# A graph kernel in three sweeps: the joint between the first and the second rearranged

## What is computed

```
h  = relu(layernorm(x))
x  = x + (adj.T @ h) * inv_deg[:, None]      # inv_deg = 1 / column sums of adj, infinite -> 0
h  = relu(layernorm(x))
x1 = silu((adj @ h)  @ W + b)
x2 = silu((adj @ x1) @ W + b)
out = x + x2
```

## Time and profile before

| | us |
|---|---|
| median of 3 runs | 663.56 (662.71 to 665.02) |
| the profiled execution | 661.49 |
| its span in the trace | 659.7 |
| busy: PE / DVE / POOL / ACT | 626.2 / 520.9 / 571.3 / 302.0 |

### The profile page before, as it was taken

One profiled execution on the slowest core, in us unless ns is written; L12 is line 12 of the kernel. 1 busy time (PEld: TensorE's weight loads), 2 busy tenths in 40 slices (PEclk: granted clock), 3 DMA queues, 4 the chain that ended last, 5 costly groups with the idle time before them and its releaser, 6 DMA issues.

```text
span 659.7 us, 6763 instructions
## 1 busy us (share of the span) xinstructions
PE 626.2 (95%) x2212; PEld 401.7 (61%) x2212; DVE 520.9 (79%) x518; ACT 302.0 (46%) x376; POOL 571.3 (87%) x287
## 2 busy tenths in 40 slices
PE   4989999999997889899999999999999999998996
PEld 2356666666564545566666666666666666665664
DVE  3988799999966879687777787787777978965982
ACT  1484442733623254646445445445435435443452
POOL 2399899599695958998999999999999999996994
PEclk9989999999998898999999999999999999999999
DMA  8999999999999699999999999909999999999971
GB/s 275 353 373 343 333 349 351 322 329 341 337 280 294 225 240 346 347 329 319 325 345 333 335 346 320 312 16 175 287 345 346 343 316 344 341 307 293 319 249 32
DMA packets 155826, 199.80 MB, mean 303 GB/s; under 512 B 5520, under 2 KB 138896, under 8 KB 155792
## 3 DMA queue, kind: packets, MB, share of 16 engines
q1 hardware_dynamic: 90512, 135.02, 65.6%
q10 hardware_dynamic: 65280, 64.36, 33.5%
HBM read 197.26 MB, written 2.10 MB: 302 GB/s over the span
## 4 chain that ended last, share of the span: by engine, by line
PE 60%; POOL 21%; issue 11%; DMA 3%; DVE 2%; ACT 1%; SPq 1%; ACTq 0%; POOLq 0%; DVEq 0%
PE dg L375 22%; POOL a_lo L738 14%; PE dg L392 10%; PE dg L381 10%; PE dg L382 10%; POOL at_lo L752 6%; PE m_ps L301 3%; PE m_ps L401 2%; DMA h<-in_x_dram 2%; DMA raw<-in_adj_dram 1%; DVE dg L591 1%; PE m_ps L306 1%; POOL norm L719 1%; PE m_ps L307 1%; PE m_ps L319 1%
## 5 line engine op out<-in xcount | busy, mean ns | idle before, releaser
L752 POOL TENSOR_TENSOR at_lo<-turned,at_hi 128x1024 fp32r<-128x1024 f32 x160 | 379.8, 2414 | 20.4 <-ACT at_hi L489 15.1
L634 DVE STREAM_TRANSPOSE turned<-raw 128x1024 f32<-128x1024 f32 x256 | 302.6, 1222 | 83.3 <-PE dg L375 40.3
L489 ACT ACTIVATE at_hi<-turned 128x1024 fp32r<-128x1024 f32 x160 | 168.6, 1059 | 196.1 <-DVE turned L634 137.6
L738 POOL TENSOR_TENSOR a_lo<-raw,a_hi 128x1024 fp32r<-128x1024 f32 x66 | 155.3, 2390 | 34.8 <-ACT a_hi L459 34.4
L375 PE MATMUL dg<-turned,f_w 128*128 128x512 f32 x384 | 181.6, 595 | 2.5 <-DVE turned L634 1.9
L591 DVE TENSOR_TENSOR dg<-raw,dg 128x2048 f32<-128x2048 f32 x60 | 137.5, 2291 | 26.2 <-DMA raw<-in_adj_dram 23.3
L381 PE MATMUL dg<-at_hi,f_hi 128*128 128x512 f32 x320 | 133.2, 416 | 4.1 <-ACT at_hi L489 4.0
L392 PE MATMUL dg<-at_lo,f_hi 128*128 128x512 f32 x320 | 130.2, 488 | 2.3 <-POOL at_lo L752 2.1
L382 PE MATMUL dg<-at_hi,f_lo 128*128 128x512 f32 x320 | 126.4, 395 | 0.0
L301 PE MATMUL m_ps<-raw,h 128*128 128x512 f32 x248 | 114.0, 606 | 10.0 <-ACT h L434 8.6
L375 PEld LDWEIGHTS dg<-turned,f_w 128*128 128x128 f32 x384 | 72.9, 190 | 58.0 <-issue 49.8
(11 more groups left out here) (48 smaller groups left out, 255.6 us busy)
## 6 DMA issues: line engine op xcount, KB each, us to landing
raw<-in_adj_dram SPq DMA_DIRECT2D x64, 1024.0 KB, 7.4
raw<-in_adj_dram ACTq DMA_DIRECT2D x122, 512.0 KB, 13.2
raw<-in_adj_dram SPq DMA_DIRECT2D x118, 512.0 KB, 12.1
x<-in_x_dram SPq DMA_DIRECT2D x16, 128.0 KB, 7.5
out_dram<-zs SPq DMA_DIRECT2D x12, 128.0 KB, 12.6
h<-in_x_dram SPq DMA_DIRECT2D x1, 768.0 KB, 9.4
h<-in_x_dram SPq DMA_DIRECT2D x1, 256.0 KB, 3.4
out_dram<-zs SPq DMA_DIRECT2D x4, 64.0 KB, 1.9
```

The lines of the kernel that those rows point to most:

```text
L489: act.activation(at_hi[:, s % RING3], turned[:, unit % TURN], ACT.Copy).then_inc(hi3_done, 1)
L634: dve.transpose(dst, src).then_inc(t3_done, 1)
L738: pool.tensor_tensor(a_lo[:, s % RING1], raw1[:, v % RAW1, i], a_hi[:, s % RING1].bitcast(f32), ALU.subtract).then_inc(lo1_done, 1)
L752: pool.tensor_tensor(at_lo[:, s % RING3], turned[:, unit % TURN], at_hi[:, s % RING3].bitcast(f32), ALU.subtract).then_inc(lo3_done, 1)
```

## The change

- WHOLE1_LAST: in the last quarter pairs 12 and 14 are whole too, so that nothing is split behind pair 11 (v = 59). In pair1 the last pair then has no rest of the pair before, and main1 takes over the end of the sum and the semaphore half_done; copy_message waits for main1_done as well.
- Memory: a_hi, a_lo, h_hi and h_lo now lie in front of raw1, and piece buffers 1 and 2, at_hi and at_lo lie over them. Pieces 1 and 2 wait for the last split pair alone (main1_done 60, its low parts, its rest1); piece 3 waits for pair 61.
- Piece 0 is issued in four places: block 0 by SP behind the load of v=53, block 1 behind that of v=55, block 2 by ScalarE behind hi1(53), block 3 behind hi1(56).
- ScalarE, behind the last split pair: its halves of pieces 1 and 2, then the rounding of units 1 and 2 (AHEAD3), then relu2(2) and the message copies; its half of piece 3 behind unit 1. GpSimd: scale_shift(2), the low parts of units 1 and 2, then lo_h2(2). GpSimd's scale_shift(2) stood behind lo1(62) before.
- The last quarter's turn_message comes behind units 1 and 7 on PE instead of 0 and 6; on DVE invert moves from unit 5 to 7, add_message from 6 and 10 to 8 and 12, node_statistics from 7 and 11 to 9 and 13.
- invert keeps the sum, its reciprocal and the comparison's result in PSUM (tp), and only the clamped value and the final inverse in SBUF.
- PE makes RISE = 14 multiplies of 128 x 128 by 128 columns, whose results nobody reads, before the first pair.

The diff, with fewer lines around each edit:

```diff
--- before.py
+++ after.py
@@ -13,9 +13,11 @@
 RAW1 = 5
+RISE = 14
 RING1 = 5
 WHOLE1 = (0, 1, 4, 7, 10, 13, 15)
+WHOLE1_LAST = (0, 1, 4, 7, 10, 12, 13, 14, 15)
 WHOLE1_FIRST = (0, 1, 2, 3, 4, 5, 7, 10, 13, 15)
@@ -41,6 +43,8 @@
 EARLY3 = (60, 61, 62, 63)
+AHEAD3 = (1, 2)
+PIECE0_SP, PIECE0_ACT = (53, 55), (53, 56)
 KEPT = range(SWEEP2, SWEEP2 + RAW3)
@@ -80,29 +84,31 @@
         norm = sb("norm", [P, 4, NT])
-        deg = sb("deg", [P, 5, QT])
+        deg, inv_deg = sb("deg", [P, QT]), sb("inv_deg", [P, QT])
         sweep1, sweep2 = ExitStack(), ExitStack()
-        raw1 = sb("raw1", [P, RAW1, 2, QC], into=sweep1)
         a_hi = sb("a_hi", [P, RING1, QC], f32r, into=sweep1)
         a_lo = sb("a_lo", [P, RING1, QC], f32r, into=sweep1)
-        h = sb("h", [P, NT, P], into=sweep1)
         h_hi = sb("h_hi", [P, 2 * len(SPLIT_ROWS), P], f32r, into=sweep1)
         h_lo = sb("h_lo", [P, 2 * len(SPLIT_ROWS), P], f32r, into=sweep1)
+        raw1 = sb("raw1", [P, RAW1, 2, QC], into=sweep1)
+        h = sb("h", [P, NT, P], into=sweep1)
         msgT = sb("msgT", [P, QC], into=sweep1)
-        raw3 = {n: sb(f"raw3_{n}", [P, GB, BC], into=sweep2) for n in (1, 2, 3)}
+        raw3 = {n: sb(f"raw3_{n}", [P, GB, BC], into=sweep2) for n in (1, 2)}
+        at_hi = sb("at_hi", [P, RING3, UC, GROUP], f32r, into=sweep2)
+        at_lo = sb("at_lo", [P, RING3, UC, GROUP], f32r, into=sweep2)
+        spare = sb("spare", [P, 512], into=sweep2)
+        raw3[3] = sb("raw3_3", [P, GB, BC], into=sweep2)
         f3_hi = sb("f3_hi", [P, UC * len(SPLIT3), P], f32r, into=sweep2)
         f3_w = sb("f3_w", [P, UC * len(WHOLE3), P], into=sweep2)
-        at_hi = sb("at_hi", [P, RING3, UC, GROUP], f32r, into=sweep2)
-        at_lo = sb("at_lo", [P, RING3, UC, GROUP], f32r, into=sweep2)
         nT = sb("nT", [P, 2, QC], into=sweep2)
         zs = sb("zs", [P, 2, QT, P], into=sweep2)
-        gap = sb("gap", [P, 3 * 1024], into=sweep2)
+        gap = sb("gap", [P, 5 * 512], into=sweep2)
         raw3[0] = sb("raw3_0", [P, GB, BC], into=sweep2)
@@ -150,7 +156,7 @@
         def whole1(v):
-            return v % PAIRS in (WHOLE1_FIRST if v < PAIRS else WHOLE1)
+            return v % PAIRS in {0: WHOLE1_FIRST, QUARTERS - 1: WHOLE1_LAST}.get(v // PAIRS, WHOLE1)
@@ -204,11 +210,15 @@
-            if i in (1, 2, 3):
-                pairs = QUARTERS * PAIRS - (2 if i == 1 else 0)
-                eng.wait_ge(main1_done, pairs)
-                eng.wait_ge(lo1_done, 2 * split_before(pairs))
-                eng.wait_ge(deg_added, pairs)
+            if i in (1, 2):
+                eng.wait_ge(main1_done, splits1[-1] + 1)
+                eng.wait_ge(lo1_done, 2 * len(splits1))
+                eng.wait_ge(rest1_done, len(splits1))
+            elif i == 3:
+                eng.wait_ge(main1_done, QUARTERS * PAIRS - 2)
+                eng.wait_ge(deg_added, QUARTERS * PAIRS - 2)
             elif i >= RAW3:
@@ -264,6 +274,8 @@
                 load1(v)
+                if v in PIECE0_SP:
+                    load3(sp, 0, SP_BLOCKS[PIECE0_SP.index(v):][:1])
                 if v % PAIRS in NODES_AT:
@@ -298,7 +310,8 @@
                     if whole1(v):
-                        mm = pe.matmul(acc, h[:, 2 * k + i], raw1[:, v % RAW1, i, cols], start=first, stop=False)
+                        last = k == PAIRS - 1 and i == 1 and whole1(v - 1)
+                        mm = pe.matmul(acc, h[:, 2 * k + i], raw1[:, v % RAW1, i, cols], start=first, stop=last)
                     else:
@@ -307,6 +320,8 @@
                     mm.then_inc(main1_done, 1)
+                elif k == PAIRS - 1 and whole1(v - 1):
+                    mm.then_inc(half_done, 1)
@@ -329,7 +344,8 @@
                         main1(v, half)
-                        rest1(v - 1, half)
+                        if before:
+                            rest1(v - 1, half)
                 else:
@@ -403,6 +419,9 @@
             pe.wait_ge(consts_ready, 1)
+            for _ in range(RISE):
+                pe.matmul(tp[:, 0, 0:P], ident[:, :], ident[:, :], start=True, stop=True)
             for v in range(QUARTERS * PAIRS):
@@ -414,9 +433,9 @@
                     rest3(unit - 1)
-                if unit == 0:
+                if unit == 1:
                     turn_message(QUARTERS - 1, 0)
-                if unit == 6:
+                if unit == 7:
                     turn_message(QUARTERS - 1, 1)
@@ -462,6 +481,7 @@
                 act.activation(turned_nodes(msgT[:, :], 0), natural(m_ps[:, 0:512]), ACT.Copy).then_inc(msgT_copied, 1)
+                act.wait_ge(main1_done, (q + 1) * PAIRS)
                 act.wait_ge(rest1_done, split_before((q + 1) * PAIRS))
@@ -481,7 +501,7 @@
                 if s == 0:
-                    act.wait_ge(main1_done, QUARTERS * PAIRS)
+                    act.wait_ge(main1_done, splits1[-1] + 1)
                     act.wait_ge(rest1_done, len(splits1))
@@ -526,17 +546,20 @@
                     relu2(v // PAIRS - 2)
-                if v // PAIRS == QUARTERS - 1 and v % PAIRS == 6:
-                    load3(act, 0, SP_BLOCKS + ACT_BLOCKS)
+                if v in PIECE0_ACT:
+                    load3(act, 0, ACT_BLOCKS[PIECE0_ACT.index(v):][:1])
+            load3(act, 1, ACT_BLOCKS)
+            load3(act, 2, ACT_BLOCKS)
+            for unit in AHEAD3:
+                hi3(unit)
             relu2(QUARTERS - 2)
-            load3(act, 1, ACT_BLOCKS)
             copy_message(QUARTERS - 1)
             for unit in range(UNITS3):
-                if not whole3(unit):
+                if not whole3(unit) and unit not in AHEAD3:
                     hi3(unit)
                 i = unit // QU + RAW3 - 1
-                if unit in (1, 2):
-                    load3(act, unit + 1, ACT_BLOCKS)
+                if unit == 1:
+                    load3(act, 3, ACT_BLOCKS)
                 if unit % QU == 0 and RAW3 <= i < len(PIECES) and i not in KEPT:
@@ -598,12 +621,13 @@
             def invert(q):
-                inv, clamped, finite, inv_deg = (deg[:, n, :] for n in range(4))
+                total, inv, finite = (tp[:, 1, n * QT:(n + 1) * QT] for n in range(3))
+                clamped = deg[:, :]
                 dve.wait_ge(msg_turned, 3 * q + 1)
-                step(dve.reciprocal(inv, tp[:, 1, 0:QT]))
+                step(dve.reciprocal(inv, total))
                 step(dve.tensor_scalar(clamped, inv, -FLT_MAX, FLT_MAX, ALU.max, ALU.min))
                 step(dve.tensor_tensor(finite, inv, clamped, ALU.is_equal))
-                dve.tensor_tensor(inv_deg, clamped, finite, ALU.mult).then_inc(inv_ready, 1)
+                dve.tensor_tensor(inv_deg[:, :], clamped, finite, ALU.mult).then_inc(inv_ready, 1)
@@ -614,7 +638,7 @@
                     ins = dve.scalar_tensor_tensor(out=row, in0=tp[:, part, m * P:(m + 1) * P],
-                                                   scalar=deg[:, 3, k:k + 1], in1=row, op0=ALU.mult, op1=ALU.add)
+                                                   scalar=inv_deg[:, k:k + 1], in1=row, op0=ALU.mult, op1=ALU.add)
                 ins.then_inc(u_ready, 1)
@@ -677,15 +701,15 @@
                 turn3(unit)
-                if unit == 5:
+                if unit == 7:
                     invert(last)
-                if unit == 6:
+                if unit == 8:
                     add_message(last, 0)
-                if unit == 7:
+                if unit == 9:
                     node_statistics(last, 0)
-                if unit == 10:
+                if unit == 12:
                     add_message(last, 1)
-                if unit == 11:
+                if unit == 13:
                     node_statistics(last, 1)
@@ -775,9 +799,12 @@
                     lo_h2(q - 2)
+            scale_shift((QUARTERS - 2) * QT, (QUARTERS - 1) * QT, len(HEAD) + QUARTERS - 2)
+            for unit in AHEAD3:
+                lo3(unit)
             lo_h2(QUARTERS - 2)
             for unit in range(UNITS3):
-                if not whole3(unit):
+                if not whole3(unit) and unit not in AHEAD3:
                     lo3(unit)
```

## The result

| | before | changed |
|---|---|---|
| median of the runs, us | 663.63 | 653.67 (652.38 to 655.49) |
| the profiled execution, us | 661.49 | 653.19 |
| its span, us | 659.7 | 651.3 |

The changed kernel takes 0.9869 of the time of before, with an interval from 0.9843 to 0.9894. The forecast was 654.4 us, with a range from 649.0 to 660.0.

A forecast was written before the change was run, and what follows sets the result against it. The prediction took late transfers plus DVE's 17.0 us chain to set sweep 2's start, then a ScalarE queue hold. Profiled 661.49 less 2.8 and 6.4 gave 652.3; the runs' median, 2.07 above, gave 654.4 us, range 649.0 to 660.0.

The forecast's parts named there:

- the joint: The turn from sweep 1 to sweep 2 and its first units: 6.4 us gained, bounds 3.9 and 7.8.
- signs that I had named for a right forecast: DVE's raw1 waits about 10 us, degs_ready near 232, no 6.40 us hold, unit 4's subtraction near 236, PE clock 1.
- Part 1: Pairs 12 and 14 whole in the last quarter: PE works 1.3 us more, covered by DVE's 17.0 us behind v=60.
- Part 2: Piece 0 in four places, last quarter: v=60 arrives 2.8 us earlier, at 214.85, so sweep 2 starts at 231.9.
- part 3: Pieces 1 and 2 issued at 219.2 instead of 227, removing 6.5 us at 53 GB/s; no gain added to 2.8.
- four signs of a wrong forecast: v=60 used no earlier than 217; first sweep-2 rounding after 230; DVE waits for piece 3 or 4; PE waits behind 280.
- Parts 3 and 4: Pieces 1 and 2 issued early; units 1 and 2 rounded ahead, ending ScalarE's 6.40 us hold: the latter gains 6.4 us.
- Parts 5 and 6: invert through PSUM (0 to 0.5 us gained) and 14 idle multiplies (0.3 lost to 1.0 gained): both taken as zero.
- The tail: Sweep 3: its 1.87 us wait at 599 for a late piece stays; bounds: gone, or 1 us longer.
- (a): Rival: last quarter runs free, nothing of piece 0's cost remains: 647.2 us, chance 0.08.
- (b): Rival: sweep 2 starts no earlier, 0.5 us later; only the 6.4 us are left: some 657.7 us, chance 0.16.
- (c): Rival: pieces 3 and 4 come late, ScalarE issuing piece 3's half only after the message copies: 661.5 us, chance 0.08.

The follow-up runs named there:

- e2: The changed kernel with piece 0's blocks issued behind v=21, 27, 37 and 43, in quarters 2 and 3 of sweep 1: 651.55 us, 0.9845 of the kernel before.
- e8: The changed kernel with the third quarter's second add_message and node_statistics on DVE behind pairs 10 and 11 instead of 12 and 13: 652.43 us.
- e9: The changed kernel with pairs 12 and 14 split again, pieces 1 and 2 waiting for the last split pair, now v=62: 661.77 us, 0.9987 of the kernel before.
- e1: The changed kernel with piece 0 issued as before, all four blocks together by ScalarE behind hi1(54): 651.55 us, 0.9834 of the kernel before.
- e1b: e1 measured again, on the chip of c1: 652.45 us, 0.9852 of the kernel before.
- c0: The changed kernel itself, unaltered, run again as control on another chip: 654.92 us, 0.9885 of the kernel before.
- e3: The changed kernel with pieces 1 and 2 waiting again for pair 61 or the last pair, as before the change: 658.40 us, 0.9954 of the kernel before.
- e7: e1 with the third quarter's second add_message and node_statistics on DVE behind pairs 10 and 11 instead of 12 and 13: 649.48 us.
- e5: The changed kernel without the 14 idle multiplies (RISE = 0): 653.45 us, 0.9855 of the kernel before.
- e6: The changed kernel with invert's intermediate values in SBUF again: 653.40 us, 0.9858 of the kernel before.
- c1: The changed kernel itself, unaltered, run a third time as control on another chip: 654.21 us, 0.9871 of the kernel before.
- e4: The changed kernel without the tiles of units 1 and 2 rounded ahead (AHEAD3 empty): 655.19 us, 0.9893 of the kernel before.

## Why the prediction was right, and where it was not

**The total** was off by 0.7 us in the median (654.4 against 653.67) and by 0.9 in the profiled execution (652.3 against 653.19). That closeness is partly luck: the start of sweep 2 brought 0.5 us instead of 2.8, the joint 7.4 instead of 6.4, and 0.6 came behind it where nothing was forecast. Against the kernel before, the forecast was 9.2 us; the ratios of the three comparisons are worth 8.7, 7.6 and 8.5 us. Of the signs that I had named for a right forecast, the waits for raw1 rose where they should have fallen to 10 us, and degs_ready (234.2 for 232) and unit 4's subtraction (237.95 for 236) came late; those of the joint (the queue's hold, PE's idle time, its clock) were there. The bounds of the sum also left out what parts 1, 5 and 6 had been given; the measurement doesn't come near them.

**Part 1**, PE's 1.3 us covered: right. Behind v=60 PE needs 15.3 us in the changed kernel (14.6 forecast), and DVE 17.0. In all profiles but e2's and e8's PE ends sweep 1 before DVE's degs_ready; in the changed kernel and its variants its wait before unit 0 is 1.2 to 3.1 us. What I did not say: the early gate of part 3 depends on this edit, as the wait follows the last split pair. I had costed it as an expense only, and e9 shows what the gate is without it.

**Part 2** is the step that failed: "v=60 arrives 2.8 us earlier, at 214.85". It was used at 217.19 in the first profile, at 214.10 and 218.11 in the next two: 1.2 us earlier on average than in the one profile of the kernel before, with a scatter of 4. So even those 1.2 us are not clear of noise. The premise was that piece 0's cost in the last quarter was an inefficiency of the burst that spreading would take back to 338 GB/s. e2 shows that most of it is not: the 2.1 MB of piece 0 cost 5.4 us of PE's time when they stand in quarters 2 and 3. e1 and e1b show that the burst is no worse than the spread. One of the four signs of a wrong forecast that I had named, v=60 at 217 or later, was there, and the gain came all the same, because the larger term doesn't depend on it. The gate of pieces 1 and 2 moved with it, to 222.30 instead of 219.2, and 2 us of the hole stayed; in c0, where v=60 was used at 214.10 and the gate opened at 218.83, no 2 us from 214 to 226 fall below 253 GB/s.

**Parts 3 and 4**: right in mechanism, the size 7.4 instead of 6.4, inside the bounds of 3.9 to 7.8. The hold of ScalarE's queue, the wait behind it and the slow clock went together; e3 shows that the early gate, with all that it sets free, carries 4.6 us of it. Between the two points in time PE's idle time fell from 6.1 to 1.3 us and the clock gave some 1.7 back; the last 0.9 us these rows don't explain. Holds have not vanished from every variant: the four blocks of pieces 1 and 2 take 5.84 us in e7, at 219.16, and piece 4's two take 3.61 there and 3.86 in e8, and yet either takes 48.0 us from unit 0 to the copy. Of the 2.1 us of waits on at_lo, of which I had left 1.4, only 1.0 stayed. Every profile with the early gate and a full clock takes 47.95 to 48.09 us from unit 0 to the copy; with a stretch at 1.2 GHz, 49.6 to 49.7. My time for unit 4's subtraction, 235.7, was 237.95: 2.3 us late, as the start was by 2.4. invert's move cost nothing that shows.

**Parts 5 and 6** at zero: right, within what a run can tell (e5, e6). **The tail**: its length is 367.9 to 370.6 in all fourteen profiles; the wait for a late piece was 1.0 to 2.8 us. I had bounded it well, but as a thing that stays; it varies.

**The rivals.** (a) did not come; in e2 the quarter runs free, and another pays. (b) is what the first profile did at the start, 0.46 us early, with a better part 4 than I gave it. (c) did not come: VectorE waits for no transfer from 234 to 290 us. Its premise was wrong too: ScalarE issued its half of piece 3 at 232.59, before the copies ran (235.87), and not behind them at 234.6. (d) did not come: ScalarE's four blocks went by 224.8; its damage, from another cause, stands in e3.

Open: what makes the last quarter's transfers scatter by 4 us between executions of one program, whether piece 0's two blocks in SP's queue cost something, and how much of the gain the whole pairs give by relieving GpSimd and ScalarE.

## What to carry to other kernels

When a phase with its own memory ends, ask which resource of it must really be finished before the next phase's first transfers can go. Here making two late pairs more expensive for PE let both queues start 11 us earlier than with the pairs split (223.00 against 233.83 us, c1 and e9), and the early start carries 4.6 of the 7.4 us won at the joint (e3), since the transfers hardly stop there any more. And before moving a load away from the place where it hurts, check that the place it goes to has spare transfer time, not only an engine without waits.

## What the runs showed that I had not expected

- Short waits can cost twice, through the clock. A wait of 2.15 or 2.16 us before unit 0 left PE at full clock in e1 and in e5, but behind one of the same length it was down to 1.2 GHz in c0, e4 and e6, where the same first four records took 2.54 to 3.64 us instead of 1.96 and the stretch to the copy was 1.5 to 1.7 us longer. In e1b even 3.09 us before unit 0 left the clock at full speed. In e3 and e9, with several waits after one another, the clock cost 3.6 and 5 us, nearly as much as the waits themselves (4.6 and 5.9 us in the view of PE's waits of either run, 233 to 290 us). The changed kernel has 3.1 us of waits there and loses no clock.
- A semaphore wait in front of a transfer holds the engine's whole list. In e3 the issues take 7.77 us from the first to the last, and two roundings stand behind them whose data were turned at 227.4 and 230.8; both start only from 234.62 on.
